# Reordering a hand-planned attention kernel: maxima among the values, projected keys in the banks of scores, other splits at the head

## What is computed

```python
q = (x @ Wq).reshape(B, S, HEADS, DIM_HEAD).transpose(0, 2, 1, 3)
k = (context @ Wk).reshape(B, L, HEADS, DIM_HEAD).transpose(0, 2, 1, 3)
v = (context @ Wv).reshape(B, L, HEADS, DIM_HEAD).transpose(0, 2, 1, 3)
attn = jnp.einsum('bhsd,bhld->bhsl', q, k) * scale
attn = jax.nn.softmax(attn, axis=-1)
out = jnp.einsum('bhsl,bhld->bhsd', attn, v)
...
x = x + _L0_xattn_ref(_layernorm(x, axis=-1), ctx_768, ...)
x = x + _L0_ffn_ref(_layernorm(x, axis=-1), ...)
```

## Time and profile before

| | us |
|---|---|
| runs | 464.14, 465.06, 468.87 |
| median | 465.06 |
| profiled execution, its own time | 468.46 |
| its span, first to last instruction | 466.6 |
| scores of pair 0 begin | 36.48 |
| values of pair 15 begin | 399.52 |

### The profile page before, as it was taken

One profiled execution on the slowest core, in us unless ns is written; L12 is line 12 of the kernel. 1 busy time (PEld: TensorE's weight loads), 2 busy tenths in 40 slices (PEclk: granted clock), 3 DMA queues, 4 the chain that ended last, 5 costly groups with the idle time before them and its releaser, 6 DMA issues.

```text
span 466.6 us, 9560 instructions
## 1 busy us (share of the span) xinstructions
PE 426.9 (92%) x3650; PEld 329.2 (71%) x3650; DVE 290.1 (62%) x596; ACT 235.6 (50%) x367; POOL 269.5 (58%) x183
## 2 busy tenths in 40 slices
PE   7998988898989988898899898989998987999997
PEld 6577674767577776666776776677767675687896
DVE  4737674748482676657633767677447595768653
ACT  4366163426167263524382627152736263589873
POOL 4404995486663185928360868291806569078982
PEclk8579997999899999899999999999999999999999
DMA  7400000200000002000000002000000000410500
GB/s 225 113 2 2 2 2 1 54 2 2 1 2 1 1 2 55 1 1 2 1 1 1 2 11 95 1 2 1 0 2 1 2 2 3 130 52 3 180 24 22
DMA packets 17139, 11.75 MB, mean 25 GB/s; under 512 B 10188, under 2 KB 14136, under 8 KB 17096
## 3 DMA queue, kind: packets, MB, share of 16 engines
q1 hardware_dynamic: 17096, 11.15, 8.8%
HBM read 10.55 MB, written 0.56 MB: 24 GB/s over the span
## 4 chain that ended last, share of the span: by engine, by line
PE 37%; DVE 12%; ACT 4%; issue 4%; POOL 3%; DVEq 0%; ACTq 0%; POOLq 0%
PE ps L1141 11%; DVE maxes L890 6%; PE ps L995 6%; PE ps L997 5%; PE ps L1126 5%; PE ps L996 5%; DVE rden L831 3%; PE ps L1071 3%; ACT probs L772 2%; POOL work L473 2%; DVE kq_lo L887 1%; POOL kq_lo L688 1%; PE ps L1024 1%; DVE work L835 1%; ACT kq_hi L733 1%
## 5 line engine op out<-in xcount | busy, mean ns | idle before, releaser
L772 ACT ACTIVATE probs<-ps 128x1024 f32<-128x1024 f32 (+1 forms) x112 | 105.8, 962 | 148.4 <-PE ps L1126 145.0
L890 DVE TENSOR_REDUCE maxes<-ps 128x1 f32<-128x402 f32 x256 | 130.9, 568 | 72.6 <-PE ps L1071 71.4
L473 POOL TENSOR_TENSOR work<-work,probs 128x1024 f32<-128x1024 f32 x60 | 142.8, 2381 | 4.7
L471 POOL TENSOR_TENSOR work<-probs 128x1024 f32<-128x1024 f32 x15 | 35.7, 2377 | 135.1 <-issue 97.6
L1141 PE MATMUL ps<-probs,v_sb 128*64 128x256 f32 (+1 forms) x832 | 98.3, 395 | 0.0
L1071 PE MATMUL ps<-kq_hi 64*128 64x402 f32 x256 | 79.2, 412 | 20.4 <-DVE maxes L890 15.4
L1126 PE MATMUL ps<-kq_hi 64*128 64x256 f32 (+1 forms) x416 | 91.2, 296 | 3.7 <-ACT probs L772 2.4
L1126 PE MATMUL ps<-kq_hi,kq_lo 64*128 64x256 f32 (+1 forms) x416 | 85.6, 280 | 0.0
L1126 PE MATMUL ps<-kq_lo,kq_hi 64*128 64x256 f32 (+1 forms) x416 | 85.5, 279 | 0.0
L1126 PE MATMUL ps<-shift_rows,ones_r 64*128 64x256 f32 (+1 forms) x416 | 85.3, 279 | 0.0
L1141 PEld LDWEIGHTS ps<-probs,v_sb 128*64 128x64 f32 (+1 forms) x832 | 60.5, 142 | 33.8 <-issue 7.7
(11 more groups left out here) (149 smaller groups left out, 634.8 us busy)
## 6 DMA issues: line engine op xcount, KB each, us to landing
v_sb<-weight_rows SPq DMA_DIRECT2D x12, 256.0 KB, 4.0
raw<-in_ctx_T_dram SPq DMA_DIRECT2D x3, 600.4 KB, 4.5
work<-in_L_ffn_rw_dram SPq DMA_DIRECT2D x1, 1024.0 KB, 7.0
shift_rows<-neg_row SPq DMA_DIRECT2D x64, 0.5 KB, 2.0
raw<-weight_rows SPq DMA_DIRECT2D x4, 256.0 KB, 3.6
raw<-in_ctx_T_dram SPq DMA_DIRECT2D x3, 150.8 KB, 2.4
x_sb<-in_x_dram SPq DMA_DIRECT2D x1, 384.0 KB, 5.6
wo_sb<-in_L_xattn_Wo_dram SPq DMA_DIRECT2D x1, 256.0 KB, 5.0
```

Of the source, the lines that this page charges most:

```text
L471: ops.tensor_tensor(acc, probs[:, (n - 1) % SLOTS], pr, ALU.add).then_inc(summed, 1)
L473: ops.tensor_tensor(acc, acc, pr, ALU.add).then_inc(summed, 1)
L772: nc.scalar.activation(dst, src, ACT.Exp, scale=SCALE).then_inc(probs_ready, 1)
L890: v.tensor_reduce(maxes[:, p % 2, i * T + t, blk:blk + 1], src[:, 0:BW], AX.X, ALU.max).then_inc(ring_taken, 1)
```

## The change

Constants: `WARM` 18 to 21, `REST_1` 4 to 3 (the `keep_awake` matmuls before and after the first transposes).

*Maxima.* Before, the 16 maxima of the next-but-one pair lay: 3 ahead of the values, 3 behind them, and 2 each behind score units 0 to 4 of the next pair. Now 8 lie among the values (2 ahead of unit 0, 4 ahead of unit 3, 2 ahead of unit 5), 2 behind them, and 2 each behind score units 1, 3 and 4. For pair 1, 10 instead of 6 precede the scores of pair 0. The DVE add is a step of its own (`add`) behind the maxima at unit 5 of the values; before it stood ahead of values unit 0, behind the 3 maxima there. The second quotient stands behind score unit 2 instead of 1.

*Projected keys.* From pair 2's on they go into the score banks instead of the ring: blocks 0 and 1 into the banks of unit 5 of the pair just scored, blocks 2 and 3 into those of unit 6. PE waits for those units' exponentials instead of a ring bank, and the next scores wait for these keys to be taken.

*Head.* POOL makes the low part of the first 128 columns of Wk (DVE did), the wait for Wq's is apart from it, the high part of Wv is made earlier, the low part of Wv ahead of the last block of the context, and `v0` steps begin earlier among the maxima.

```diff
+AMONG_VALUES = ((0, 2), (3, 4), (5, 2))
+BEHIND_VALUES = 2
...
-        ahead = maxima[n + 1][2 * EARLY_MAXIMA:] if n + 1 < n_order else []
+        ahead = maxima[n + 1][before_scores:] if n + 1 < n_order else []
...
-            out += ahead[:2]
...
+            if n and u in (behind, behind + 2):
+                out.append(("quotient", order[n - 1] + ((u - behind) // 2,)))
+            if u in (1, 3, 4):
+                out += ahead[:2]
...
-        out += following[:EARLY_MAXIMA]
-        out += [("values", (b, p, u, j)) for u, unit in enumerate(key_units(chunks)) for j in range(len(unit))]
+        for u, unit in enumerate(key_units(chunks)):
+            for at, count in AMONG_VALUES:
+                if u == at:
+                    out += following[:count]
+                    following = following[count:]
+            if u == AMONG_VALUES[-1][0] and n:
+                out.append(("add", (b, p)))
+            out += [("values", (b, p, u, j)) for j in range(len(unit))]
...
-        out += following[EARLY_MAXIMA:2 * EARLY_MAXIMA]
+        out += following[:BEHIND_VALUES]
...
+            if w[0] == "k" and n > kinds.index("scores"):
+                last = (w[1] * PAIRS + w[2] - 1) * NU - 1
+                ring_banks.append(2 * ((last - (w[3] < 2)) % 2) + w[3] % 2)
...
-            for i in range(BLOCKS):
+            pool.wait_ge(w0_hi_ready, 1)
+            g.tensor_tensor(wk_lo[:, 0:P], wk_sb[:, 0:P], wk_hi[:, 0:P].bitcast(F32), ALU.subtract).then_inc(w0_ready, 1)
+            for i in range(3):
                 low_part(0, i)
...
+            low_part(0, 3)
...
-                if kind == "values" and w[2:] == (0, 0) and w[:2] != (0, 0):
-
+                if kind == "add":
                     add_probabilities(v, dve, then_own, (w[0], w[1], NU - 1))
...
+                        pair = b * PAIRS + w[2]
+                        if pair >= 2:
+                            pe.wait_ge(probs_ready, (pair - 1) * NU - (w[3] < 2))
```

More of the change, by code:

```diff
@@ L70, in plan @@
         out += [x] + rest[2 + i:3 + i]
-    out += rest[2 + len(second):] + maxima[1][:2 * EARLY_MAXIMA]
+    out += rest[2 + len(second):] + maxima[1][:before_scores]
     for n, (b, p) in enumerate(order):
-        ahead = maxima[n + 1][2 * EARLY_MAXIMA:] if n + 1 < n_order else []
+        ahead = maxima[n + 1][before_scores:] if n + 1 < n_order else []
         behind = 2 if n == 1 else 0
@@ L77, in plan @@
             out.append(("scores", (b, p, u)))
-            out += ahead[:2]
-            if ahead and len(ahead) <= 2:
-                out.append(("shift", order[n + 1]))
-            ahead = ahead[2:]
+            if n and u in (behind, behind + 2):
+                out.append(("quotient", order[n - 1] + ((u - behind) // 2,)))
+            if u in (1, 3, 4):
+                out += ahead[:2]
+                if ahead and len(ahead) <= 2:
+                    out.append(("shift", order[n + 1]))
+                ahead = ahead[2:]
             if (n, u) == (1, 1):
                 out.append(("sums", order[0]))
-            if n and u in (behind, behind + 1):
-                out.append(("quotient", order[n - 1] + (u - behind,)))
         vs = [("ring", ("v", b, c)) for c in range(chunks)] if p == 0 and b else []
@@ L212, in build @@
             lowest = 2 if n < kinds.index("scores") else 4 if n < kinds.index("first") else 5
+            if n > kinds.index("scores") and not early_last:
+                early_last.update(held)
+            if w[0] == "k" and n > kinds.index("scores"):
+                last = (w[1] * PAIRS + w[2] - 1) * NU - 1
+                ring_banks.append(2 * ((last - (w[3] < 2)) % 2) + w[3] % 2)
+                ring_last.append(None)
+                continue
             bank = min(range(lowest, O_BANK), key=lambda i: held.get(i, -1))
@@ L216, in build @@
             held[bank] = k
-    LAST_OF = [max((k for k, bank in enumerate(ring_banks) if bank == i), default=0) for i in range(O_BANK)]
+    LAST_OF_4 = max(k for k, bank in enumerate(ring_banks) if bank == 4)
     hi_no = {w: i for i, w in enumerate(w for w in ring_list if w[0] in ("k", "q"))}
@@ L1109, in _ @@
                         for bank in (2, 3):
-                            pe.wait_ge(*taken(ring_list[LAST_OF[bank]]))
+                            pe.wait_ge(*taken(ring_list[early_last[bank]]))
                     if u == 0:
-                        pe.wait_ge(*taken(("k", b, p, BLOCKS - 1)))
+                        following = (b * PAIRS + p + 1) // PAIRS, (p + 1) % PAIRS
+                        pe.wait_ge(*taken(("k",) + ((b, p) if pair in (0, B * PAIRS - 1) else following) + (BLOCKS - 1,)))
                         pe.wait_ge(s_shift[pair], 64)
```

32 lines of the change are left out of this document (17 added, 15 removed).

## The result

The changed kernel takes 482.56 us (median of four runs, 481.99 to 490.64) against 464.6 for the kernel before on the same chip: ratio 1.0366, 95% interval 1.0282 to 1.0449. The change costs 18 us. I forecast 473.0, with 458 to 481 as the range. The direction is right, the size is not, and the time lies outside the range. The profiled execution took 482.44, its span 480.3.

The account below looks back on a forecast made before the run. PE, busy 92%, was taken stage by stage: waiting on DVE and ACT in scores, DVE in projections, nothing in values. Terms -2.4 + 3.7 - 1.3 + 6.2 - 3.1 + 5.3 = +8.4 on the 465.06 median gave 473 us, range 458 to 481.

Parts of the forecast that it names:

- Scores stage: Scores of a plain pair: five maxima fewer, PE and ACT become the bound; 8.3 us against 9.73, -1.4.
- Projections: Projections of a plain pair: nothing in the ring waits for DVE any more; 3.0 us against 5.09, -2.1.
- Values stage: Values to next scores, plain pair: fourth maximum waits for a bank, row sums for the add; 9.2 us against 6.48, +2.7.
- Pairs 6 and 10: Late add delays their first exponential to 5.5 to 6.1 us into scores; +3.1 each, plus +2 each for lower clock.
- Pair 0: Ten maxima ahead of the first scores and longer waits among its values, less the projections' gain: +3.7.
- Pair 1: PE waits in this pair for normalised tokens whatever the keys do: 0.
- Head: Start of the kernel: PE starts 1.2 us earlier, mostly at 1.2 GHz, some v0 steps fill waits: -2.4.
- this rival: The clock holds in the head because keep_awake and early keys remove idle: -10.7 instead of -2.4, 465 us; chance 0.20.
- Clock: Two stretches at 0.50, from 120.16 and 195.25, lose the projections' waits ahead of them and go: -3.1.
- Row sums that do not wait: Values stage: row sums find the add done and added idle does not lower the clock; -18, 455 us; chance 0.20.
- The wait for exponentials eats the ring's gain: Projections: keys wait for ACT as long as for DVE before; 20 more whole, a quarter gives 478 to 482; chance 0.08.
- Nothing happens: Whole kernel: PE and DVE totals stay, waits only change places; 465 to 469 us; chance 0.05.

Follow-up runs that it names:

- The last experiment: Changed kernel with DVE add before the last two values maxima, normalisation behind the fourth score unit, six maxima before pair 0, values maxima placed 2, 3, 3: 439.2 us.
- the normalisation experiment: Changed kernel with ACT's normalisation of the next tokens moved behind the fourth unit of scores in pairs 6 and 10: 470.4 us, ratio 1.006.
- the add first: Changed kernel with the DVE add moved ahead of the last two maxima among the values instead of behind them: 459.3 us, ratio 0.990.
- the order alone: Kernel before with only the new order of v0 steps, the value weights' split and x's blocks; keep_awake and Wk/Wq low parts as before: 465.5 us, ratio 0.9925.
- the split alone: Kernel before with only POOL making the low part of Wk's first columns, DVE only Wq's: 471.5 us, ratio 1.014.

## Why the prediction missed

**The mechanism was right, its largest terms were not sized right.** From the profiled execution the sum was +8.4; measured is 13.7 in span. The terms in its order:

- *Scores stage* -1.4, 8.3 us: measured 8.17. *Projections* -2.1, 3.0 us: measured 3.09. Both right.
- *Values stage* +2.7, 9.2 us: **this step failed in size**, 9.90. The maxima 7 and 8 enter 6.11 us into it, not 5.65: 24 values took 2.74 instead of 2.6, the four maxima 1.50 instead of 1.3, 16 values 1.87 instead of 1.74. The chain behind them took 2.92, as forecast 2.9. From the sums to the next scores it was 0.87, not 0.6; the earlier trace rows have 0.82 there, with three maxima. So +3.4, and the 0.7 recur in every pair: with the same size in pairs that I put at 0 (`y`, `v`) they make most of the +7.9 over pairs 2 to 13. I took 0.109 a value from a run of 52 and applied it to pieces of 24, 16 and 12. The last experiment shows the bare price: 7.91 for 52 values, eight maxima and the sums, without a wait, against 6.48 with three maxima. Of the 1.43 between, the six maxima among the values are 1.12 (three in 0.56), and the 52 values in three pieces take 5.97 instead of 5.66 in one: 0.31 for two interruptions, about 0.15 each. The 5.66 of the earlier trace rows had no interruption, so the row bounded that price from neither side, and I gave it no range.
- *Pairs 6 and 10* +3.1 each, and +2 each for the clock: measured +4.5 in pair 6 (the stretch from 195.25, which lay in it before, is gone) and +5.6 in pair 10. The first exponential came 5.1 into the scores, not 5.5 to 6.1. The mechanism is shown by the normalisation experiment: 12 us by the medians, 13.0 in the two pairs of the profiles, against my 12.6.
- *Pair 0* +3.7: measured +5.9. I did not expect the clock to fall in it. Six maxima ahead of the scores instead of ten take 4.1 back. *Pair 1* 0: measured +1.7; its sums too wait for the late add (of the 2.5 that it gained with the add first, half are that), which I had not counted.
- *Head* -2.4: measured -8.3. I gave this rival 0.20, by the idle ahead of 7.52, and put it down to `keep_awake` and early keys. The outcome came, and with it one of my signs of being wrong; pair 0's scores began 5.7 earlier, not "no earlier". The reason fell: the clock holds without the longer `keep_awake`, and the early low part alone does not hold it; the order of v0 does. The rival's price of 10.7 was 2.4 too high.
- *Clock* -3.1: the stretches from 120.16 and 195.25 were gone, as said, but such stretches come in some executions and not in others: the order alone, with the same waits in pairs 3 and 6, had none in either, the split alone one in each. So their going is luck at least in part. I took them off and also took the median as base, which is 3.4 lower than the execution that had them. **One of the two was right, not both.** That alone is 3.4 of the miss of 9.6.

In sum, measured less predicted: pairs 2 to 13 +7.9, pairs 0 and 1 +3.9, head -5.9, pairs 14 and 15 and the rest -0.6, makes the 5.3 between 8.4 and 13.7; base and rounding give the rest. The head hid a larger error: had I known that it holds, I would have said 465.

**The rivals.** *Row sums that do not wait* would have been 455: that is what moving the add gives, 459.3, so rival and forecast split at the right place. *The wait for exponentials eats the ring's gain* did not come in the changed kernel: the first key waits 0.55 us, and a plain pair's projections are shorter by 2.0. With the keys moved alone it did, in ten of fourteen pairs. Its price was added up wrongly: 2.1 in 14 pairs are 29 us, not 20. *Nothing happens* was wrong for the total, but right for the plain pair by accident: 21.16 against 21.30.

## What to carry over

Splitting a dense run of matmuls costs at each seam (here about 0.15 us), and one step placed last among equals on another engine can be worth more than the whole change (here 22 us against 18): look at the idle time that the consumer's engine has just ahead of it, and put the step that someone waits for there. Fill no more at a time than the ring has banks, and count what else holds one. Base and credits must come from the same execution: a slow stretch that is only in the profiled one may be taken off its time, not off the median.

## What the runs showed of the hardware

VectorE and GpSimd: the low part of Wq's first 128 columns took DVE 1.11 us beside POOL's context split, and 0.28 while POOL stood still. DVE and POOL of the changed kernel:

```profile
5.30 0.28 DVE L878 TENSOR_TENSOR w_all<-early,w_all 128x128 fp32r<-128x128 f32 x1
```

```profile
4.59 0.45 POOL L632 TENSOR_TENSOR w_all<-early,w_all 96x128 fp32r<-96x128 f32 x1
5.77 3.05 POOL L628 TENSOR_TENSOR ctxT_lo<-raw,ctxT_hi 96x402 fp32r<-96x402 f32 x3 [0.73 <-ACT ctxT_hi L722]
```

POOL of the kernel before, beside DVE's 6.27 to 7.38:

```profile
5.10 2.13 POOL L612 TENSOR_TENSOR ctxT_lo<-raw,ctxT_hi 96x402 fp32r<-96x402 f32 x2 [0.44 <-ACT ctxT_hi L703]
```

POOL's second block ended at 7.23, DVE's instruction 0.15 later. The traces speak for its having stood until POOL was done, and not for its having run slowly: in the eleven other profiled executions in which a low part of Wk or Wq took 1.12 to 1.14, it ended 0.15 behind a block of POOL's too, and that block took no longer than 1.03 in most of them, as in the changed kernel without DVE beside it. The Trainium skill, SBUF — State Buffer, section SBUF: two separate sides, says that for a VectorE instruction with two SBUF inputs beside a GpSimd one that reads SBUF the shared port is an exclusive lock held for the whole instruction; the trace agrees (1.11 against 0.28). I had read the 1.11 as the price of the operation; it was the price of its moment. The new order does not avoid it: of thirteen profiled executions with Wk's low part on POOL, Wq's took 0.28 in four, in which POOL's context split began at 5.50 or later, and 1.12 to 1.14 in nine. With the keys moved alone, in the old order, both low parts took 0.28, POOL's split beginning at 5.42.

The granted clock of TensorE differs between executions of one kernel. Head or order alone ranged over 16 and 12 us in ten runs each, and stretches at 0.50 came in pairs 6, 11 and 15 in some profiles and not in others. What decides it in a given execution stays open.
